# A four-layer graph network on one core: ScalarE's dense work dealt out in pieces, index making moved beside another stage, two VectorE steps exchanged

## What is computed

```
# layer 1: ten hops
out = x
for _ in range(10):
    out = segment_sum(out[col] * w[:, None], row) * 0.9 + x * 0.1
# layer 2: graph convolution, with self loops
h = x @ W
out = segment_sum(h[row] * dinv[row] * dinv[col], col) + b
out = where(out >= 0, out, prelu_a * out)
# layer 3: Chebyshev terms of degree 1 to 3, mixed by attention, batch norm
prop = lambda h: segment_sum(wn[:, None] * h[row], col)
# layer 4: relu(x[src] + e) summed at dst, two dense layers, twice
```

## Time and profile before

| | |
|---|---|
| median of 3 runs | 13920.73 us (13897.24 to 13924.33) |
| profiled execution | 13921.51 us, span 13919.8 us |
| TensorE busy, weight load busy | 5477.0 us (39%), 4357.4 us (31%) |
| VectorE busy | 7700.5 us (55%) |
| ScalarE busy | 4324.3 us (31%) |
| GpSimd busy | 8089.8 us (58%) |
| mean granted TensorE clock | 0.664 of full speed |

### The profile page before, as it was taken

The page is one execution under the profiler, slowest core; times in us unless marked ns, Lnnn a source line. Parts: engine busy times, 40 slices in busy tenths (PEclk is TensorE's granted clock), DMA queues, the critical chain, the costliest instruction groups (busy, mean ns, idle before and its releaser), DMA issues. The chain is left out here.

```text
span 13919.8 us, 114314 instructions
## 1 busy us (share of the span) xinstructions
PE 5477.0 (39%) x29175; PEld 4357.4 (31%) x29175; DVE 7700.5 (55%) x13539; ACT 4324.3 (31%) x11110; POOL 8089.8 (58%) x8280
## 2 busy tenths in 40 slices
PE   0000002100000000210003877776778888988876
PEld 0000002000000000210002666654556887766544
DVE  8880245444444444542256255676755778567753
ACT  0000011100000000110046565466655246654654
POOL 0567777777777777777733773177765000721767
PEclk9965555555555555555556767987789988999555
DMA  7300124434334334431257544444467788876743
GB/s 227 117 4 3 36 78 137 123 113 119 113 113 119 113 113 119 127 107 53 55 187 239 167 142 132 148 141 126 138 212 244 233 288 316 269 252 227 227 165 111
DMA packets 955756, 2071.60 MB, mean 149 GB/s; under 512 B 318458, under 2 KB 323856, under 8 KB 938977
## 3 DMA queue, kind: packets, MB, share of 16 engines
q1 hardware_dynamic: 689376, 1702.87, 35.4%
q0 software_dynamic: 265728, 361.43, 11.6%
HBM read 1251.36 MB, written 822.13 MB: 149 GB/s over the span
## 5 line engine op out<-in xcount | busy, mean ns | idle before, releaser
L720 POOL DMA_INDIRECT hop_raw<-hop_table,i_hop x2352 | 2219.6, 944 | 734.5 <-issue 693.0
L814 PE MATMUL hop_rows<-hop_chain,src_carries 128*128 128x96 f32 x12 | 4.3, 450 | 3023.8 <-DVE hop_chain L790 3023.8
L744 DVE TENSOR_TENSOR hop_rows<-hop_raw,hop_factors 128x672 f32<-128x672 f32 x336 | 289.9, 863 | 1494.4 <-DMA hop_raw<-hop_table,i_hop 1494.4
L822 ACT ACTIVATE hop_keeps<-src_inner 128x672 f32<-128x672 f32 x336 | 255.4, 762 | 2665.2 <-DVE hop_chain L790 2613.1
L516 POOL DMA_INDIRECT gine_raw<-x,i_near x392 | 379.1, 967 | 1177.4 <-POOLq L89 1058.2
L516 POOL DMA_INDIRECT cheb_raw<-cheb_table,i_cheb x784 | 817.4, 1043 | 244.9 <-issue 235.9
L814 PEld LDWEIGHTS hop_rows<-hop_chain,src_carries 128*128 128x128 f32 x12 | 3.0, 312 | 3025.1 <-issue 3025.1
L516 POOL DMA_INDIRECT cheb_raw<-x,i_near x392 | 446.4, 1139 | 510.0 <-POOLq L89 390.8
L516 POOL DMA_INDIRECT gine_raw<-conv,i_near x392 | 387.6, 989 | 603.6 <-POOLq L89 484.5
L1784 POOL DMA_INDIRECT own_raw<-x,i_dst x392 | 370.1, 944 | 505.3 <-POOLq L89 386.2
L1621 PE MATMUL cheb_base_product<-folded,cheb_base_turned_rows 97*128 97x292 f32 x1568 | 561.9, 514 | 177.1 <-ACT cheb_base_mixed L1580 177.1
(11 more groups left out here) (560 smaller groups left out, 22128.9 us busy)
## 6 DMA issues: line engine op xcount, KB each, us to landing
...
```

The lines of the kernel that those rows point to most:

```text
L720: pool.indirect_dma_start(out=raw_rows[:, b % RAW, g, :], out_offset=None, in_=table, in_offset=bass.IndirectOffsetOnAxis(ap=index[:, t:t ...
L744: nc.vector.tensor_tensor(by_channel(b).rearrange("p c t -> p t c"), raw[:, b % RAW, :, :], spread(weights[:, at], C), ALU.mult).then_inc( ...
L814: nc.tensor.matmul(carried, side.carries[:, :], chain[:, (batches - 1) % LINES, :, EDGE - 1], start=True, stop=True).then_inc(s["carried"], 1)
L822: nc.scalar.activation(keeps[:, b % LINES, :, :], side.inner[:, b * EDGE:(b + 1) * EDGE].unsqueeze(1).to_broadcast([P, C, EDGE]), ACT.Copy ...
```

## The change

1. In `hop_pass`, for the last batch alone, `add(b - 1)` stands ahead of `weigh(b)`.
2. In `edge_pass` the first job's copy and relu are pieces (`PIECES = 2` for `GcnRows`, 0 for all other jobs) that are dealt to four places of a batch: behind the first and the second part of the sums, and behind the first and the second part of the weighed rows. The norm stays at the batch's end. Jobs without pieces are issued as before.
3. The three small stages are gone. Their instructions are a job `ChebIndex` of 8 steps beside "gcn_slots", so that one of its steps stands behind each thirteenth step.

```diff
--- before.py
+++ after.py
@@ -605,6 +605,13 @@
 
         @block.scalar
         def _(act):
+            def early(b, part):
+                for job in jobs[0:1 if jobs and jobs[0].PIECES else 0]:
+                    steps = share(job, b, batches)
+                    count = len(steps) * job.PIECES
+                    for u in range(part * count // (2 * len(PARTS)), (part + 1) * count // (2 * len(PARTS))):
+                        job.scalar_early(ph, act, steps[u // job.PIECES], u % job.PIECES)
+
             def take_root(b):
                 act.wait_ge(s["met"], 2 * b + 2)
                 nc.scalar.activation(root[:, b % WORK, :], degree[:, b % WORK, :], ACT.Sqrt).then_inc(s["rooted"], 1)
@@ -616,8 +623,10 @@
                     take_root(b)
             for b in range(batches):
                 h, w = b % RAW, b % WORK
-                if jobs and b:
-                    finish.scalar(ph, act, b - 1)
+                for q in range(len(PARTS)):
+                    if jobs and b:
+                        finish.scalar_part(ph, act, b - 1, q)
+                    early(b, q)
                 if added is not None:
                     act.wait_ge(s["joined"], b + 1)
                 else:
@@ -637,11 +646,15 @@
                             ins = nc.scalar.activation(rows[:, w, g, :], raw[:, h, g, :], ACT.Copy,
                                                        scale=weight[:, t:t + 1])
                     ins.then_inc(s["weighed"], 1)
+                    early(b, len(PARTS) + q)
                 if not jobs:
                     finish.scalar(ph, act, b)
                 for job in jobs:
                     for q in share(job, b, batches):
-                        job.scalar(ph, act, q)
+                        if job.PIECES:
+                            job.scalar_late(ph, act, q)
+                        else:
+                            job.scalar(ph, act, q)
             if jobs:
                 finish.scalar(ph, act, batches - 1)
             act.wait_ge(s["chained"], batches * STEPS)
@@ -771,9 +784,13 @@
                 job.vector_setup(ph, dve)
             for b in range(batches):
                 t = b * EDGE
-                weigh(b)
-                if b and finish.residual is not None:
+                if b == batches - 1 and finish.residual is not None:
                     add(b - 1)
+                    weigh(b)
+                else:
+                    weigh(b)
+                    if b and finish.residual is not None:
+                        add(b - 1)
                 dve.wait_ge(s["weighed"], b + 1)
                 if b:
...
-    def scalar(self, ph, act, q): pass
+    def scalar_early(self, ph, act, q, n): pass
+
+    def scalar_late(self, ph, act, q):
+        self.scalar_norm(ph, act, q)
+
+    def scalar(self, ph, act, q):
+        for n in range(self.PIECES):
+            self.scalar_early(ph, act, q, n)
+        self.scalar_late(ph, act, q)
+
...
-    normed, width, after_turn, held = True, WIDE, "product", 3
+    normed, width, after_turn, held, PIECES = True, WIDE, "product", 3, 2
...
 
-    def scalar(self, ph, act, q):
+    def scalar_early(self, ph, act, q, n):
         s = q + 1
-        self.copy(ph, act, q + 2, True)
-        if 0 <= s < 2 * self.count:
+        if n == 0:
+            self.copy(ph, act, q + 2, True)
+        elif 0 <= s < 2 * self.count:
             act.wait_ge(self.sem(ph, "hidden"), s + 1)
             if s >= 2:
                 act.wait_ge(self.sem(ph, "product"), s - 1)
             self.nc.scalar.activation(self.hidden_rows[:, s % 2, :, :], self.hidden[s % self.banks][:, :, :], ACT.Relu,
                                       bias=self.c0[:, 0:1]).then_inc(self.sem(ph, "activated"), 1)
...
 
     def scalar(self, ph, act, b):
+        for q in range(len(PARTS)):
+            self.scalar_part(ph, act, b, q)
+
+    def scalar_part(self, ph, act, b, q):
         e, s = ph.edge, ph.sems
-        self.slot_free(ph, act, b)
-        for q, (g0, n) in enumerate(PARTS):
-            bank = e["total"][b % e["sets"] * len(PARTS) + q]
-            act.wait_ge(s["chained"], b * STEPS + g0 + n + 1)
-            if e["scale"] is not None:
-                for g in range(g0, g0 + n):
-                    ins = self.nc.scalar.activation(e["sums"][:, b % WORK, g, :], bank[:, g - g0, :], ACT.Copy,
-                                                    scale=e["scale"][:, b * EDGE + g:b * EDGE + g + 1])
-            else:
-                ins = self.nc.scalar.activation(e["sums"][:, b % WORK, g0:g0 + n, :], bank[:, 0:n, :], ACT.Copy)
-            ins.then_inc(s["copied"], 1)
+        g0, n = PARTS[q]
+        if q == 0:
+            self.slot_free(ph, act, b)
+        bank = e["total"][b % e["sets"] * len(PARTS) + q]
+        act.wait_ge(s["chained"], b * STEPS + g0 + n + 1)
+        if e["scale"] is not None:
+            for g in range(g0, g0 + n):
+                ins = self.nc.scalar.activation(e["sums"][:, b % WORK, g, :], bank[:, g - g0, :], ACT.Copy,
+                                                scale=e["scale"][:, b * EDGE + g:b * EDGE + g + 1])
+        else:
+            ins = self.nc.scalar.activation(e["sums"][:, b % WORK, g0:g0 + n, :], bank[:, 0:n, :], ACT.Copy)
...
+class ChebIndex:
+
+
+    SEMS = ["index_own", "index_degrees", "index_rooted"]
+    steps = range(8)
...
+    def vector(self, ph, dve, q):
+        nc, k, own, met = self.nc, self.k, self.own, self.met
+        if q == 0:
+            own.step(nc.vector.tensor_scalar(self.nowhere[:, :], k.lane[:, :], float(k.EP + P + 1), None, ALU.add))
+            own.step(nc.vector.tensor_copy(self.far[:, :], self.node[:, :]))
+            own.step(nc.vector.tensor_scalar(self.near[:, :], met[:, :, 2], 0.0, None, ALU.is_ge))
+            own.wait()
+        elif q == 1:
+            own.step(nc.vector.tensor_scalar(self.lost[:, :], met[:, :, 2], 0.0, self.nowhere[:, 0:1], ALU.is_lt, ALU.mult))
+            own.step(nc.vector.scalar_tensor_tensor(self.step[:, :], met[:, :, 2], float(k.NP), self.far[:, :],
+                                                    ALU.add, ALU.subtract))
+            own.wait()
+        elif q == 2:
+            own.step(nc.vector.tensor_tensor(k.i_cheb[:, :], met[:, :, 2], self.lost[:, :], ALU.add))
+            own.step(nc.vector.tensor_tensor(self.step[:, :], self.step[:, :], self.near[:, :], ALU.mult))
+            own.wait()
+        elif q == 3:
+            own.step(nc.vector.tensor_tensor(k.i_near[:, :], self.far[:, :], self.step[:, :], ALU.add))
             for n, degree in enumerate((met[:, :, 1], k.own_degree[:, :])):
+                own.step(nc.vector.tensor_scalar(self.deg[:, n, :], degree, 1.0, None, ALU.max))
+                own.step(nc.vector.tensor_scalar(self.has[:, n, :], degree, 0.0, (1.0, -1.0)[n], ALU.is_gt, ALU.mult))
+            own.wait()
+            dve.sem_inc(ph.sems["index_degrees"], 1)
+        elif q == 5:
+            dve.wait_ge(ph.sems["index_rooted"], 1)
+            own.step(nc.vector.reciprocal(self.inv[:, :, :], self.root[:, :, :]))
+            own.wait()
+        elif q == 6:
             for n, weight in enumerate((k.w_cheb, k.f_cheb)):
+                own.step(nc.vector.tensor_tensor(weight[:, :], self.inv[:, n, :], self.has[:, n, :], ALU.mult))
+
+    def vector_end(self, ph, dve):
+        self.own.wait()
+
+    def scalar(self, ph, act, q):
+        if q == 4:
+            act.wait_ge(ph.sems["index_degrees"], 1)
+            self.nc.scalar.activation(self.root[:, :, :], self.deg[:, :, :], ACT.Sqrt).then_inc(ph.sems["index_rooted"], 1)
 
 
 class Features:
...
-        find_rows(nc, k, "cheb_rows", k.i_cheb, by_dst.met[:, :, 2])
-        find_nearest(nc, k, k.i_near, by_dst.other, by_dst.met[:, :, 2])
-        prepare_cheb(nc, k, by_dst.met)
-        slot_rows(nc, k, "gcn_slots", GcnRows(nc, k, "ends", False, slots, x1_slots, *layer, x2_slots, sums=hop_a))
+        slot_rows(nc, k, "gcn_slots", GcnRows(nc, k, "ends", False, slots, x1_slots, *layer, x2_slots, sums=hop_a),
+                  (ChebIndex(nc, k, by_dst.met, by_dst.other),))
 
 
```

58 lines of the change are left out of this document (18 added, 40 removed).

## The result

The changed kernel takes 13904.93 us (median of 12 runs), the kernel before 13921.06 us in the same rounds. The ratio is 0.9984, 95% interval 0.9976 to 0.9992: 11 to 33 us are gained, 16 by the medians, which is 0.12%. The forecast was 13906. One run of the twelve, 14109 us, was disturbed and is not in the ratio.

A forecast was written before the change was run, and what follows sets the result against it. It took a ScalarE-VectorE loop and TensorE's clock-dependent steps to bound the gather, and a strict TensorE-VectorE ring "gcn_slots". 13921.5 - 6 (hops) + 7 (small stages and slots) - 16 (gather) gave 13906 us, range 13870 to 13944.

The forecast's parts named there:

- -6 (hops): Hops: moving the add into the wait for the last gather saves 0.76 us in each of eight passes.
- +7 (small stages and slots): Removed stages -16.1 us, uncovered VectorE pieces in "gcn_slots" +7.0, low-clock spells +16: net +7, from -9 to +13.
- -16 (gather): Second layer's gather: spreading copy and relu gains 16 us, bounds 29 us gained and 9 us lost.
- rival 4: Hops: the earlier store delays the last rows, so the moved add gains nothing; 13912 us, chance 0.05 together with others.
- piece 3: "gcn_slots": five VectorE index instructions, 2.1 us, behind an odd step whose 1.81 us wait covers all but 0.3.
- 3.5 spells at 4.5 us: "gcn_slots": longer TensorE waits make its clock fall 3.5 times, each costing 4.5 us; 16 us in all.
- Rival (1): Kind clock: gather at its loops (-29), "gcn_slots" keeps 2.4 GHz (-9), hops -6; 13877 us, chance 0.19.
- I take 10.5 us in A and 9.55 in B: Gather batch times after the change, for odd step last (A, before 10.98) or even step last (B, before 9.75).
- Both loops: Gather: the ScalarE-VectorE loop per batch grows from 9.15 to 10.19 us in A and stays 9.35 in B.
- The lead of some 3.5 us: Gather, pattern A: TensorE's second product is ready some 3.5 us before VectorE asks, covering most of a low-clock spell.
- (2): Re-dealing gives nothing: gather 0 to +9 us, behind it +7 to +13, hops -6; 13922 to 13938 us, chance 0.22.
- (3): TensorE stays at 1.2 GHz all through the gather, 12.06 us per two-step batch; 14004 us, chance 0.08.

The follow-up runs named there:

- after_again: The changed kernel timed and profiled once more, with nothing altered, on the chip of the single-part runs; ratio 0.9993 to the kernel before.
- gather_only: The kernel before with only the re-dealing of copy and relu in the second layer's gather; ratio 0.9987 to the kernel before, gather 559.4 us.

## Why the prediction was right

**The sum.** Forecast -15.5 us against the profile, 13906; measured 13904.93. The terms were -6 (hops), +7 (small stages and slots) and -16 (gather). The profiles give -5.2, +6.1 and -32.5, single parts timed give -6, +14 and -18. Averaged over all profiles with and without each part they are -5, +9 and -26, so -22 in all, where the forecast said -15. That the median came within about 1 us of the forecast is therefore partly luck: it moved by 16 us here and by 14 for after_again, within intervals of some 10 us either way, and by the profiles the forecast gave the gather 10 us too little.

**The hops.** Mechanism right, term slightly too large. 0.76 us was the step between two starts. The bridge that follows reads the weighing's result and now starts 0.90 us after the weighing does, just behind its 0.86 us, where before the add had hidden that wait. It is 0.64 us a hop and 5.1 in all; the last rows' delay (rival 4) was seen only as 0.3 to 0.4 us in one or two hops.

**The slots.** Right in place and size. VectorE's direct share was forecast at 7.0 us and is 6.75 (7.1 with the one wait that has no piece); the hidden pieces are hidden; piece 3 is 0.33 over, as forecast, and the reciprocal 3.19 instead of 3.3. 3.5 spells at 4.5 us made 16; three at 5.0 are 15.1, and four in after_again gave some 23. Stage forecast 395, measured 393.8 to 402.1. (The 14 us a spell that this was worked out from were 13.7, 20.5 and 13.7 us in the trace of before.) The granted clock was forecast under 0.9 and came out at 0.92 and 0.89. Rival (1)'s half on the slots, a kind clock, did not come.

**The gather.** Mechanism right and the mis-sized term of the sum: the step "I take 10.5 us in A and 9.55 in B". Both loops were foreseen to the hundredth (10.19 and 9.35; measured 10.18 and 9.34), and so was the wait of 3.9 us for weighed rows, but the stage sits on them at either clock. The lead of some 3.5 us is there too (3.4 at the high level). I let only "most" of a low spell be covered, since I added TensorE's idle at the start of a spell to what it loses in it; the lead carried nearly every spell. (The recorded reading that the clock fell in the gap of 2.79 us is off by a little: that gap ended at 8271.60, and the low level began at 8272.38.) What remains are a few batches of B that come second in a low stretch (11.0 to 11.8 us) in four of the other profiles and none in the changed kernel's own, which explains 553 against 556 to 559. The five profiles with this dealing mean 557.1 us and the three full kernels with the old one 583.0: -26 us, where I said -16 and gave -29 as the bound. The gather's half of rival (1), a stage at its loops, thus came nearly true, though without a kinder clock. Timed alone, the part is worth -18 with an interval of -31 to -6, which holds both.

**The rivals.** (2), that the re-dealing gives nothing, is refuted by gather_only. (3), TensorE cold throughout at 12.06 us a batch, did not come: the mean clock was 0.70 to 0.72 in the five profiles with the new dealing and 0.67 to 0.71 in the three with the old. "More high clock" in B, which I had called likely, is thus hardly seen. The Trainium skill, TensorE: Matmul & The Clock Gate, section "A second HAM failure mode: psum-queue depth-cycling", says that the clock swings with frequent short idles. The rows agree as far as that (it does swing in every kernel here, and cutting the waits from 2.79 to 1.94 us did not stop it), but a swing is not the clock that stays low which (3) needed, and its cost did not appear, because the swing no longer reaches the loop.

**Why the median moved less than the profile.** The gain of 40 us between two profiled executions is 32 us of change and 8 us of later stages that wander by themselves. The 32 us are a fortunate pair too: the profile of before has the longest gather of the three with the old dealing (585.7, else 579.3 and 584.1), and that of the changed kernel the shortest of the five with the new one. By stage, after_again shows 18 us of change. The average of -22 and the medians of -16 and -14 agree within their intervals.
